# Attention's products with V in one run a pair, the output weight made mean-free, and the last tile's splits inside its turn

## What is computed

```python
x = L0_attn_X
xn = _layernorm(x, axis=-1)
# attention, 16 heads, D = 64: Q and K have two halves each
P = softmax(Q1 @ K1.T / 8) - lam * softmax(Q2 @ K2.T / 8)
O = P @ V
Y = concat(O) @ Wo + bo
mu, var = mean(Y), var(Y)                       # over the 256 columns
attn = ((Y - mu) * rsqrt(var + 1e-5) * gamma + beta) * 0.2
# experts: of 8, the one with the largest route probability
ffn = prob_max * (gelu(xn @ w1[e] + b1[e]) @ w2[e] + b2[e])
return x + attn + ffn
```

## Time and profile before

| | us |
|---|---|
| median of 3 runs | 1855.72 (1851.82 to 1857.77) |
| the profiled execution | 1859.52 |
| its span, first to last instruction | 1857.7 |
| attention, about 50 to 1474 us of the span | 1424 |
| feed-forward, to about 1738 | 264 |
| output, to the end | 120 |

### The profile page before, as it was taken

One profiled execution on the slowest core, in us unless ns is written; L12 is line 12 of the kernel. 1 busy time (PEld: TensorE's weight loads), 2 busy tenths in 40 slices (PEclk: granted clock), 3 DMA queues, 4 the chain that ended last, 5 costly groups with the idle time before them and its releaser, 6 DMA issues. The chain is left out here.

```text
span 1857.7 us, 32559 instructions
## 1 busy us (share of the span) xinstructions
PE 1795.7 (97%) x10474; PEld 1397.3 (75%) x10474; DVE 1549.6 (83%) x2585; ACT 1405.4 (76%) x3307; POOL 693.7 (37%) x774
## 2 busy tenths in 40 slices
PE   5899999999999999999999999999999999999896
PEld 4676777777777777777777777777777799999896
DVE  7888888888888888888888888888999766666588
ACT  6798888888888888888888888888788766666311
POOL 4444223333233332233323333222237455555543
PEclk9999999999999999999999999999999999998898
DMA  9998888888888888888888888888887576667897
GB/s 313 261 244 229 236 225 215 216 229 226 212 217 226 220 221 221 225 221 218 223 216 211 216 226 231 214 215 230 216 214 185 195 281 240 237 230 233 261 315 243
DMA packets 212908, 427.68 MB, mean 230 GB/s; under 512 B 28080, under 2 KB 107952, under 8 KB 206736
## 3 DMA queue, kind: packets, MB, share of 16 engines
q1 hardware_dynamic: 208064, 412.24, 79.9%
q0 software_dynamic: 4688, 13.51, 2.4%
HBM read 175.17 MB, written 49.15 MB: 121 GB/s over the span
## 5 line engine op out<-in xcount | busy, mean ns | idle before, releaser
L633 ACT ACTIVATE e<-p_score,nmax 128x512 f32<-128x512 f32 x1024 | 697.3, 689 | 128.7 <-DVE nmax L930 128.4
L930 DVE TENSOR_REDUCE nmax<-p_score 128x2 f32<-128x1024 f32 x512 | 623.4, 1218 | 166.9 <-PE p_score L1058 166.1
L480 POOL TENSOR_SCALAR e<-e,rrec,lam 128x512 f32<-128x512 f32 x512 | 393.6, 769 | 951.6 <-DVE rrec L890 951.3
L1058 PE MATMUL p_score<-ks,qs 128*128 128x512 f32 x2048 | 578.8, 404 | 9.3 <-DMA ks<-k_parts 6.3
L1058 PEld LDWEIGHTS p_score<-ks,qs 128*128 128x128 f32 x2048 | 365.5, 188 | 179.8 <-ACT e L633 53.5
L897 DVE SCALAR_TENSOR_TENSOR pm<-e,rrec 128x512 f32<-128x512 f32 x512 | 394.0, 770 | 0.2 <-POOL e L480 0.2
L1021 PE MATMUL p_proj<-xh,w 128*128 128x512 f32 x1024 | 386.4, 418 | 6.0 <-POOL xl L458 4.6
L565 ACT COPY pT<-p_tr 128x512 f32<-128x512 f32 x512 | 301.1, 588 | 113.4 <-PE p_tr L1070 113.1
L1070 PE MATMUL p_tr<-consts,pm 128*128 128x128 f32 x2048 | 308.8, 273 | 1.3 <-ACT pT L565 1.2
L1070 PEld LDWEIGHTS p_tr<-consts,pm 128*128 128x128 f32 x2048 | 249.7, 140 | 79.1 <-issue 19.6
L1085 PE MATMUL p_pv<-pT,v 128*64 128x512 f32 x1024 | 247.7, 605 | 0.7 <-ACT pT L565 0.7
(11 more groups left out here) (192 smaller groups left out, 1875.0 us busy)
## 6 DMA issues: line engine op xcount, KB each, us to landing
ks<-k_parts SPq DMA_DIRECT2D x512, 256.0 KB, 4.7
qs<-q_parts SPq DMA_DIRECT2D x512, 128.0 KB, 4.5
w<-weight_parts_scratch SPq DMA_DIRECT2D x56, 1024.0 KB, 10.8
w<-in_w SPq DMA_DIRECT2D x46, 1024.0 KB, 7.4
oT_parts_scratch<-oT SPq DMA_DIRECT2D x32, 512.0 KB, 6.3
op<-oT_parts_scratch SPq DMA_DIRECT2D x32, 512.0 KB
wv<-weight_parts_scratch SPq DMA_DIRECT2D x56, 256.0 KB, 5.5
weight_parts_scratch<-w SPq DMA_DIRECT2D x8, 1024.0 KB, 6.1
```

The lines of the kernel that those rows point to most:

```text
L480: nc.gpsimd.tensor_scalar(e2, e2, rrec[:, g % 4, 1:2], lam[:, 0:1], ALU.mult, ALU.mult).then_inc(s_e2, 1)
L633: nc.scalar.activation(ex[:, g % EX, m, :], p_score[g % 2][:, m, :], ACT.Exp, bias=nmax[:, g % 2, m:m + 1], accum_out=rsum[:, g % 4, m:m + ...
L930: vec.tensor_reduce(nmax[:, g % 2, :], p_score[g % 2][:, :, :], AXX, ALU.max, negate=True).then_inc(s_max, 1)
L1058: last_op = nc.tensor.matmul(p_score[g % 2][:, m, :], qs[j][u][:, m, qt * P:(qt + 1) * P], ks[j][u][:, m, part, :], start=(part == 0), sto ...
```

## The change

In attention the products with V of a pair are made in one run of sixteen at place 5, for the pair before. The projections stand at places 0, 1, 3, 6, V at 2. `copy_o`, `low_o` move to place 7 of the same pair, on ScalarE behind `high_part` and ahead of `copy_pT`; SP's store of o goes behind the copies of k1.

In the feed-forward stage `output_weights` is cut in portions that run behind turns 11 to 16. It now also subtracts from each row of `wo`, and from the bias row, its mean over the 256 columns, so that the products come out with mean zero. The loop over turns ends two turns sooner. In the last turn, behind the second group of gelus, ScalarE copies the high part of one half of w2 and VectorE makes both parts of the other half.

In the output stage the mean is no longer needed: ScalarE squares and sums each half group (`square`), VectorE makes 1/sqrt of the mean square in six small steps, multiplies a whole group by gamma in one instruction (`times_gamma`), and the last two groups are finished one by one instead of as a pair.

```diff
-        AT_STEP = {0: "q0", 2: "k0", 4: "q1", 6: "k1"}
-        V_STEP = 3
-        PV_FIRST, PV_LAST = 5, 1
+        AT_STEP = {0: "q0", 1: "k0", 3: "q1", 6: "k1"}
+        V_STEP, PV_STEP, O_STEP = 2, 5, 7
...
-                if pair >= 2:
-                    store_o(pair - 2)
...
+                if 1 <= pair < NPAIRS - 1:
+                    store_o(pair - 1)
...
-                if st == 2 and pair >= 2:
-                    copy_o(pair - 2)
                 what = AT_STEP.get(st - 1)
                 if what and pair + 1 < NPAIRS:
                     high_part(pair + 1, what)
+                if st == O_STEP and 1 <= pair < NPAIRS - 1:
+                    copy_o(pair - 1)
                 if g >= LAG:
                     copy_pT(g - LAG)
...
-                if st == 2 and pair >= 2 and not whole(pair - 2):
-                    low_o(pair - 2)
+                if st == O_STEP and 1 <= pair < NPAIRS - 1 and not whole(pair - 1):
+                    low_o(pair - 1)
...
-                if st == PV_FIRST and 1 <= pair < NPAIRS - 1:
-                    times_v(pair - 1, (0, 1))
-                if st == PV_LAST and pair >= 2:
-                    times_v(pair - 2, (2, 3))
+                if st == PV_STEP and 1 <= pair < NPAIRS - 1:
+                    times_v(pair - 1, range(QT))
...
+        OUT_TURNS = [(n, n + 1) for n in range(0, GROUPS - 2, 2)] + [(GROUPS - 2,), (GROUPS - 1,)]
+        STEPS_OF_TURN = 6
+        WO_FROM = 11
...
-        LOOP_END = PAIR_TILES // 2 - 2
+        LOOP_END = PAIR_TILES // 2 - 3
...
                     if g == X_AT and t.first():
                         x_high(1, 1, True, FS)
+                    if g == X_AT and not t.has(1):
+                        act.wait_ge(s_w2[j], 16 * (t.half + 1))
+                        nc.scalar.copy(w2p[j][:, 0, 0:HALF_F, :], w2[j][:, 0:HALF_F, :]).then_inc(s_w2hi, 1)
...
+            def output_weights(n):
+                if n == WO_FROM + 3:
+                    act.wait_ge(s_centred, 3)
+                    nc.scalar.copy(wop[:, 0, :, :], wo[:, :, :]).then_inc(s_wohi, 1)
+                    nc.scalar.copy(bop[:, :], rows[:, 0, :]).then_inc(s_wohi, 1)
+                    act.wait_ge(s_ones, 1)
+                    nc.scalar.copy(ones_r[:, :], ones[:, :]).then_inc(s_wohi, 1)
+                elif n == WO_FROM + 5:
+                    act.wait_ge(s_bo, 2)
+                    nc.scalar.copy(bop[:, :], bo_rows[:, :]).then_inc(s_wohi, 1)
...
-            turns(body, after_third=output_weights)(act)
+            turns(body, after=output_weights)(act)
...
+            def square(n, i, k):
+
+                act.wait_ge(s_oy, n + 1)
...
+                    nc.scalar.activation(squares[s], p_o[n % R][:, s, :], ACT.Square,
+                                         accum_out=mom[i % 2][:, 0, 2 * k + s:2 * k + s + 1]).then_inc(s_sq, 1)
...
+                    if g == X_AT and not t.has(1):
+                        dve.wait_ge(s_w2[j], 16 * (t.half + 1))
+                        own, rest = w2p[j][:, :, HALF_F:FT, :], w2[j][:, HALF_F:FT, :]
+                        v.tensor_copy(own[:, 0, :, :], rest).then_inc(s_w2hi_dve, 1)
+                        dve.wait_ge(s_w2hi_dve, 1)
+                        v.tensor_tensor(own[:, 1, :, :], rest, own[:, 0, :, :].bitcast(F32), ALU.subtract
+                                        ).then_inc(s_w2lo_dve, 1)
...
+                elif n in (WO_FROM + 2, WO_FROM + 3):
+                    a = half * (n - WO_FROM - 2)
+                    v.tensor_tensor(wo[:, a:a + half, :], wo[:, a:a + half, :],
+                                    wo_mean[:, a:a + half].unsqueeze(2).to_broadcast([P, half, E]), ALU.subtract
+                                    ).then_inc(s_centred, 1)
...
-            turns(body, after_third=output_weights)(dve)
-            dve.wait_ge(s_w2hi, FFN_TILES)
-            v.tensor_tensor(w2p[0][:, 1, HALF_F:FT, :], w2[0][:, HALF_F:FT, :], w2p[0][:, 0, HALF_F:FT, :].bitcast(F32),
-                            ALU.subtract).then_inc(s_w2lo_dve, 1)
+            turns(body, after=output_weights)(dve)
...
+            def times_gamma(n):
+
+                r = n % R
+                dve.wait_ge(s_sq, 2 * n + 2)
...
+                v.tensor_tensor(acc[r][:, :, :], p_o[r][:, :, :], gamma.unsqueeze(1).to_broadcast([P, 2, E]), ALU.mult
+                                ).then_inc(s_t, 1)
```

More of the change, by code:

```diff
@@ L1248, in ffn_and_output_stage @@
         ff = [[sb(f"ff{r}{s}", [P, E]) for s in range(2)] for r in range(R)]
-        ostats = [sb(f"ostats{a}", [P, 4, 6]) for a in range(2)]
+        squares = [y[1][:, s, :] for s in range(FS)]
         mom = [sb(f"omom{a}", [P, 6, 4]) for a in range(2)]
+        wo_mean, bo_mean = sb("wo_mean", [P, PAIRS]), sb("bo_mean", [P, 1])
         warm = ahead.warm
@@ L1264, in ffn_and_output_stage @@
         s_wohi, s_wolo, s_bo = sem("o_wohi"), sem("o_wolo"), sem("o_bo")
+        s_mean, s_centred = sem("o_mean"), sem("o_centred")
         s_op, s_of = [sem(f"o_op{c}") for c in range(OPS)], [sem(f"o_of{c}") for c in range(2)]
@@ L1318, in has, with turns @@
                 return self.n + k < FFN_TILES if self.exact else True
-        def turns(body, before_last=None, after_third=None):
+        def turns(body, before_last=None, after=None):
             def run(engine):
@@ L1333, in run @@
                     body(Turn(n, n % 2, n // 2, True))
+                    if after:
+                        after(n)
             return run
@@ L1666, in step @@
                     ins_.then_inc(s_d, 1)
-                    dve.wait_ge(s_d, MOMENT_STEPS * q + done[0])
-                    if done[0] == RECIPROCAL_STEP:
-                        if 2 * q + OPS < GROUPS:
-                            low_o(2 * q + OPS)
-                        base(2 * q)
-                        base(2 * q + 1)
-                for c in range(2):
-                    n = 2 * q + c
-                    dve.wait_ge(s_oy, n + 1)
-                    for s in range(2):
-                        last_op = v.bn_stats(ostats[a][:, 2 * c + s, :], p_o[n % R][:, s, :])
-                    last_op.then_inc(s_bn, 1)
-                dve.wait_ge(s_bn, 2 * q + 2)
-                moments_first(nc, step, ostats[a], mom[a])
-                moments_second(nc, dve, step, mom[a], s_root, q + 1)
-                for c in range(2):
-                    normed(2 * q + c)
-                if 2 * q + OPS + 1 < GROUPS:
-                    low_o(2 * q + OPS + 1)
-                for c in range(2):
-                    result(2 * q + c)
+                    dve.wait_ge(s_d, STEPS_OF_TURN * i + done[0])
+                last = groups[-1]
+                for n in groups[:-1]:
+                    times_gamma(n)
+                    if n > 0:
+                        base(n)
+                    if n + OPS < GROUPS:
+                        low_o(n + OPS)
+                dve.wait_ge(s_sq, 2 * last + 2)
+                step(v.tensor_scalar(ve, total, 1.0 / E, EPS, ALU.mult, ALU.add))
+                step(v.reciprocal(rec, ve))
+                times_gamma(last)
+                if i == 0:
+                    base(0)
+                base(last)
+                if last + OPS < GROUPS:
+                    low_o(last + OPS)
+                dve.wait_ge(s_root, i + 1)
+                step(v.tensor_tensor(dif, near, near, ALU.mult))
+                step(v.tensor_tensor(dif, dif, ve, ALU.mult))
+                step(v.tensor_scalar(dif, dif, -0.5, 1.5, ALU.mult, ALU.add))
+                step(v.tensor_tensor(rstd, near, dif, ALU.mult))
+                assert done[0] == STEPS_OF_TURN
+                for k, n in enumerate(groups):
+                    result(n, m, k)
         @block.tensor
```

99 lines of the change are left out of this document (55 added, 44 removed).

## The result

The changed kernel takes **1940.77 us** (median of 4 runs, 1931.53 to 1945.94) against 1855.18 us for the kernel before on the same chip: ratio 1.0462, 95% interval 1.0437 to 1.0486. It is 4.6% slower; 1867 was forecast, range 1843 to 1884. The profiled execution has a span of 1944.1 us, 86.4 more than the 1857.7 before.

| stage | before, us | after, us | difference | forecast |
|---|---|---|---|---|
| attention | 1474.5 | 1565.8 | +91.4 | +16 |
| feed-forward | 263.7 | 266.7 | +3.0 | +1.5 |
| output | 119.5 | 111.5 | -8.0 | -5.5 |

What follows compares the result with a forecast made beforehand. Attention was taken as one serial list of TensorE work, the output stage's middle as paced by loads. 16.1 - 3.9 + 5.9 - 0.5 - 5.5 = +12 gave 1867 us against the median of 1855.7; range 1843 to 1884.

Steps and rivals of the forecast that it cites:

- D: Rival, attention: four projections in a row don't fit, st1 to st4 lose 0.12 each; +30, 1897 us; chance 0.05.
- The order of the engines: Attention: one V run -27.3, copy_o at st7 +34.7, second bare step +8.7; together +16 us.
- loss 1: Attention: copy_o at st7 delays copy_pT and so S(1) by 0.56 a pair, 62 times; +34.7 us.
- Loss 2: Attention: a second bare step, st4, makes st5 wait for copy_pT, 0.14 a pair, 62 times; +8.7 us.
- Rival B: Attention: copy_o hides, its 34.7 falls away; 1832 us, faster; chance 0.17.
- The gain of 0.44 a pair: Attention: one run of V products costs 3.86 instead of 4.30 for two, 62 pairs; -27.3 us.
- Output weight: Feed-forward: turn 3's stop goes, -3.9; TensorE waits 4.2 near turn 15 and the clock adds 1.7, +5.9.
- Last tile: End of feed-forward: sooner w2 splits, partly offset by GpSimd and VectorE taking turns; -0.5 us (bounds -2.6 and 0).
- Output stage: Output: middle paced by loads gains nothing, tail -4.9, first loads sooner 0.6; -5.5 us (bounds -4 and -13.5).
- Rival C: Output stage is paced by TensorE: -13.5 instead of -5.5; 1859 us, no measurable change; chance 0.18.

Runs made afterwards that it cites:

- e3_w_load_later: The change with the load of w moved behind the next pair's q0 and k0 copies on SP's queue; 1869.46 us, ratio 1.0081.
- e5_store_back: The change with the store of oT back behind the copies of k0, ahead of the load of wv; 1870.64 us, ratio 1.0085.
- e8_half_w_bytes: The change with the load of w bringing 0.5 MB instead of 1 MB a pair, for timing alone; 1868.39 us, ratio 1.0076.
- e11_one_run_alone: The kernel before with only a pair's V products in one run of 16 at place 5; 1903.19 us, ratio 1.0271.
- e12_rest_wop_halves: Kernel before with the change's feed-forward and output stages, output weight's high part copied in halves behind turns 14 and 15; 1844.53 us, ratio 0.9958.
- e15_extra_store: The kernel before with 0.5 MB more written to HBM ahead of the load of w for 46 pairs; 1958.19 us, ratio 1.0554.
- e13_extra_ahead: The kernel before with 0.5 MB more read from HBM ahead of the load of w for 46 pairs; 1868.54 us, ratio 1.0057.

## Why the prediction was right or wrong

**The step that failed** is one sentence on attention: on SP's queue q1's copies a step sooner, k1's in the same place, "and store_o behind instead of ahead of them: nothing". It was some +70 us: e3_w_load_later, e5_store_back and e8_half_w_bytes, in which the stops are gone, are 70 to 72 us under the change, and e18_w_then_store, which only swaps the store and the load, 64 under it. Of the 75 us by which attention missed its forecast 59 are waits for ks (65.4 over the span, 6.3 before); the lower clock behind them, not priced here, is a part of the rest. I had asked whether the store makes SP wait, and not what it does to the transfers behind it. The earlier trace rows had the warning, a DMA share of 0.85 at 221 GB/s in the stage that I called one serial list of TensorE work. In the pair shown the last of k0's copies landed 1.0 us ahead of the next pair, and over pairs 9 to 60 of that trace 1.6 in the median: a second list with a margin of 1.6 us, which I never worked out. No rival named it; D, the slow one, was about ScalarE and VectorE.

**The order of the engines** was right. e3_w_load_later and e8_half_w_bytes, which take the stops away, end attention at 1489.9 and 1489.2, 15.5 and 14.8 behind the kernel before, where +16 was forecast. st0 is 3.34 (some 3.4 forecast), st4 1.28, st5 5.16 to 5.24 (5.1). On ScalarE the copy to oT stands where it was put:

```profile
677.57 0.69 ACT L553 ACTIVATE k_parts<-p_proj,bias 128x512 fp32r<-128x512 f32 x1
678.13 0.59 ACT L571 COPY oT<-p_pv 128x512 f32<-128x512 f32 x1
678.60 0.61 ACT L564 COPY pT<-p_tr 128x512 f32<-128x512 f32 x1
```

From its start to the next copy's it holds ScalarE for 0.47, not 0.56, and 0.47 is also what st0 gives back when it moves to st6: loss 1 was 29, not 34.7. Loss 2 was 8 to 13 and not 8.7 (st5 against the 5.03 of a bare step with one run behind it), so a part of the agreement in the sum is luck. Rival B (1832) is refuted by st0; the wait that spoke against it in the earlier trace rows is that of the matmul, not of the weight load of the earlier trace rows, but the conclusion held. D is refuted too: in a pair without a stop st1 to st3 are 2.75 to 2.83.

**The gain of 0.44 a pair** holds only as part of the change; alone it turns into a loss of 0.78 (e11_one_run_alone). I had priced the second bare step with the change's own spacing, which was the right case.

**The range.** The forecast's own bounds add up to 1849 to 1880, so the 1884 at its upper end came from nowhere, and 1855.7 + 12 is 1868, not 1867. Neither matters beside the 70 us.

**Output weight.** TensorE and the two engines ahead of it in turn 15, in order of time:

```profile
1734.91 4.62 POOL L1453 TENSOR_TENSOR w2p<-w,w2p 128x2048 fp32r<-128x2048 f32 x1 [5.15 <-ACT w2p L1515]
...
1737.67 2.95 DVE L1654 TENSOR_TENSOR wo<-wo,wo_mean 128x1024 f32<-128x1024 f32 x1
...
1740.65 1.90 ACT L1524 CAST wop<-wo 128x2048 fp32r<-128x2048 f32 x1 [5.82 <-DVE wo L1654]
...
1743.84 5.49 PE L1765 MATMUL p_h<-xsp,w1p 128*128 128x256 f32 x24 [4.09 <-ACT h L1502]
```

The wait is 4.09 (4.2 forecast), by the chain described: VectorE's subtraction ends at 1740.62, 1.1 behind GpSimd's end at 1739.53, as the row of 3.10 in the earlier trace rows did. The Trainium skill (SBUF — State Buffer, Who interferes with whom) has the two exclude each other; the trace agrees, with 2.95 us for work that ends 1.1 behind GpSimd. The products behind the wait take 2.6 more than 2.88, the granted clock being at its lower level; I had taken 1.7. The stop of turn 3 is gone. The price was confirmed from the other side: e12_rest_wop_halves takes this stop away and gains 5.6 where 6.7 stood in the rows. The parts measured, -3.8 for turn 3, +6.7 here and -1.5 for the last tile, make +1.4; the other 1.6 of the stage's +3.0 were not located.

**Last tile.** TensorE starts its products with w2p after 3.17 idle instead of 3.54, and they take 4.36 instead of 5.49. I had -0.5; it is -0.4 and 1.1 more by the clock:

```profile
1828.37 4.36 PE L1781 MATMUL p_y<-w2p,hp 128*128 128x256 f32 x24 [3.17 <-DVE hp L1609]
```

**Output stage.** -8.0 against -5.5, both terms mis-sized. The last product and VectorE's last row:

```profile
1931.30 2.99 PE L1808 MATMUL p_o<-wop,op 128*128 128x256 f32 x24
...
1937.11 0.88 DVE L1703 SCALAR_TENSOR_TENSOR acc<-acc,omom,x 128x256 f32<-128x256 f32 x2
...
1940.48 0.88 DVE L1703 SCALAR_TENSOR_TENSOR acc<-acc,omom,x 128x256 f32<-128x256 f32 x2
```

The tail is 1941.4 - 1934.3 = 7.1 long, 2.5 less than before and not 4.9: the last group waits for the one before it, whose result VectorE writes at 1937.11. The middle gained the other 5.5, where I had 0.6, because I took it to be paced by loads alone. From its first product to its last the stage moved 295 GB/s before, at a share of 0.92, and 328 after, at 0.99; in the 80 us that begin 22 us behind the first product it was 323 (1.00) and 348 (1.05). Before, VectorE held TensorE up too: 4.0 us in two waits for the low part of op, which VectorE makes (`low_o`). TensorE in order of time, before:

```profile
1804.64 0.35 PE L1752 MATMUL p_o<-bop,ones_r 128*128 128x256 f32 x1 [2.25 <-DVE op L1619]
1832.70 0.36 PE L1752 MATMUL p_o<-bop,ones_r 128*128 128x256 f32 x1 [1.73 <-DVE op L1619]
```

After, with bn_stats gone from VectorE, there is no such wait: TensorE waits only for loads of op, 3.5 us in total (0.9 before). In all its idle time in the stage fell from 8.2 to 3.8 us and its busy time by 1.0, since a stretch at the lower clock from 1759.3 on came only before. That VectorE's lighter work is what let the middle shrink is read from these waits; no run isolates it. The Trainium skill (DMA: Bandwidth & Descriptors, Specifications) has some 358 GB/s as a core's limit at HBM; the trace's 348 over those 80 us is close to it. Rival C had a size of 8 for the middle; its mechanism was not what happened, since the share rose and TensorE still waits for loads.

## What to carry to other kernels

Ask of every moved DMA not only who waits for it, but which transfers stand behind it on its queue, when they land, and when they are due; a stage with TensorE at 100% and a DMA share of 0.85 has two lists to keep, and the margin of the second must be worked out as carefully as the first. Here a store to HBM with a big load directly behind it, ahead of copies that were due, cost some 70 us; moving either away gave it back, and swapping the two lines gave 64 us. Nor does a DMA share of 1.00 prove that loads alone set the pace: in the output stage TensorE waited for VectorE as well. A single tile between a copy and its store ties the copy's place to the store's, and bare steps may only be added where the engines that follow TensorE have had time to catch up.

## What the runs showed of the hardware

- 0.5 MB more ahead of a load of 1 MB cost 103 us as a store (e15_extra_store) and 11 us as a read of bytes that the load itself fetches next (e13_extra_ahead), over 46 pairs; the load landed in 12.3 and 9.0 us, and in 10.8 with nothing added.
- Order decides: the store behind the load instead of ahead of it took the waits for ks from 65.4 to 19.5 us (e18_w_then_store).
- The DMA share is time, not bytes. Attention moved 221 GB/s at 0.85 before, 209 at 0.87 after and 241 at 0.90 with the extra read; full queues moved 213 GB/s at 1.09 in the 10 us shown, and 348 at 1.05 in the output stage.
- Behind a stop of 4.6 us TensorE's granted clock was at its lower level (1.2 GHz) until 5.7 us after the products began again, behind one of 4.1 us until 5.5 after: st0 took 5.29 instead of 3.34, and 24 products 5.49 instead of 2.88 in turn 15.
